# The first quarter of each batch normalisation is centred ahead of its power, and one high part moves to VectorE

## The chip, the cores and the metric

The kernel runs on one core of one Trainium2 chip. The metric is the device time of one execution in microseconds: the median of three runs. One execution was also profiled, and all rows below come from it. Names: PE is TensorE, DVE is VectorE, ACT is ScalarE, POOL is GpSimd, SP is SyncE, and PEld is TensorE's loading of weights.

## The reference, cut to what matters

The input is 8 images of 64 channels and 16 x 16 pixels. Four layers follow each other: two attention layers, a block with two batch normalisations and two convolutions with binary weights, and a whitening layer. The change touches the third and, slightly, the fourth.

```python
def batch_norm(x, gamma, beta):
    mean = jnp.mean(x, axis=(0, 2, 3), keepdims=True)
    var = jnp.mean((x - mean) ** 2, axis=(0, 2, 3), keepdims=True)
    xhat = (x - mean) * jax.lax.rsqrt(var + EPS)
    return xhat * gamma[None, :, None, None] + beta[None, :, None, None]

out = jax.nn.relu(batch_norm(x, gamma0, beta0))
shortcut = x
out = conv3x3(out, quantize_w1bit(w0))        # E * sign(w), E = mean(|w|)
out = jax.nn.relu(batch_norm(out, gamma1, beta1))
out = conv3x3(out, quantize_w1bit(w1))
return out + shortcut
# then layer 4: a mean, a 4x4 covariance per channel group, its Cholesky factor,
# a triangular solve, a mix with small weights and a bias
```

## The kernel before, in words

**Layout.** The 128 partitions hold 2 groups of 64 channels (`lanes(0)` and `lanes(1)`), each with 4 of the 8 images. The free dimension is 1024 columns: 4 quarters of 256, so one quarter is one image of each group. Every engine has its own queue of instructions, written out by hand in program order; semaphores are the only link between them. No planner orders anything.

**Attention** ends with a loop over eight units on every engine. In its tail DVE adds the shortcut of unit 6 and unit 7 (`add_shortcut`, L846), takes statistics of each quarter (L852), and between them computes for both normalisations a power of two from gamma and beta (`power_of_two`, L783 to L789), which POOL needs for the binary weights (`taps`, L373).

**A normalisation** (n = 0 on the attention's output in SBUF, n = 1 on the first convolution's output in PSUM) runs so. DVE aggregates the statistics (L923), PE combines both groups (`combine`, L666 and L667), DVE forms the variance (L929, L931), POOL raises it to the power -1/2 (L380), and DVE forms a scale `bn_s` (L935) and a shift `bn_b` (L936). Meanwhile DVE takes the absolute sums of the weights of both convolutions (`weight_sum`, L800), which PE averages (L721).

**The inputs of the convolution** are split, because the matmul reads 16-bit operands: for each quarter and each group there is a high part (the normalised, clipped value rounded to 16 bits) and a low part (the 32-bit value less the high part). They go into padded tiles `conv_in`, the high part into one half of the partitions and the low part into the other. For quarter 0, ACT writes both high parts (L473, L479) while DVE computes the 32-bit value (L902, then clipping in L903) and both low parts (L911). For quarters 1 to 3, ACT writes the clipped 32-bit value `act32` (L476) and the high part of group 1 (L479); DVE copies the high part of group 0 (L906) and subtracts its low part (L911); POOL subtracts the low part of group 1 (L386). In the second normalisation, quarter 0 was first copied out of PSUM by ACT (`z0`, L457).

**The convolution** of a quarter (`conv`, L675) is 18 matmuls and starts when its low parts are there: `lo0_out` from DVE, and `lo1_first` from DVE for quarter 0 or `lo1_out` from POOL for the others. PE works through the quarters in order. `keep_warm` (L527) fills PE's waits with matmuls of zeros. Between the convolutions, DVE takes statistics of each quarter of the first (L918). In the second, DVE takes the statistics of quarter 0 (L961, L962) between the parts of quarters 1 and 2, and PE averages them ahead of quarter 2 (L735); ACT waits for that before it centres the shortcut (L484, L488).

**After it** DVE adds the shortcut (L968), PE transposes the four quarters (L700), ACT copies each out (L494), PE multiplies each with itself (`gram`, L708), and a chain of small steps on DVE leads to the final weights and four last matmuls (L764).

Of the kernel before, what the change touches and what calls it, by code (L numbers as in the profile page):

```python
# [22 lines left out]
P = 128  # L23
B, C, H, W = 8, 64, 16, 16
G = 2
# [87 lines left out]
def build(nc, x, attn_w, params, consts, select, conv_w, out):  # L113
    with ExitStack() as ctx:
# [43 lines left out]
        z0 = sb("z0", [P, N])  # L158
# [67 lines left out]
        var_out, rstd_out, bn_out = sem("var_out"), sem("rstd_out"), sem("bn_out")  # L226
        act_out, hi0_out, hi1_out = sem("act_out"), sem("hi0_out"), sem("hi1_out")
        lo0_out, lo1_out, lo1_first = sem("lo0_out"), sem("lo1_out"), sem("lo1_first")
# [87 lines left out]
        def _(pool):  # L316
# [58 lines left out]
            for n in range(2):  # L375
# [6 lines left out]
                for q in range(1, PAIRS):  # L382

                    pool.wait_ge(act_out, n * (PAIRS - 1) + q)
                    pool.wait_ge(hi1_out, n * PAIRS + q + 1)
                    nc.gpsimd.tensor_tensor(padded(conv_in[n][1], lanes(0), q), img(act32[lanes(1), quarter(q)]),  # L386
                                            padded(conv_in[n][1], lanes(1), q), ALU.subtract).then_inc(lo1_out, 1)
# [5 lines left out]
        def _(act):  # L393
# [59 lines left out]
            for n in range(2):  # L453
                if n == 1:

                    act.wait_ge(stats_out, 1)
                    nc.scalar.activation(z0[:], pb_conv[0][0][:, 0:N], ACT.Identity).then_inc(z0_out, 1)  # L457
                act.wait_ge(bn_out, n + 1)
                for q in range(PAIRS):
                    src = xs[LAYERS][:, quarter(q)] if n == 0 else pb_conv[0][q][:, 0:N]  # L460
                    if n == 1 and q == 0:
                        act.wait_ge(z0_out, 1)
                        src = z0[:]
                    if n == 1:

                        act.wait_ge(lo0_out, q + 1)
                        if q >= 1:
                            act.wait_ge(lo1_out, q)
                    if q == 0:

                        act.wait_ge(pads_set, 4)
                        rows = lanes(0)
                        nc.scalar.activation(padded(conv_in[n][0], rows, q), img(src[rows]), ACT.Relu,  # L473
                                             scale=bn_s[n][rows], bias=bn_b[n][rows]).then_inc(hi0_out, 1)
                    else:
                        nc.scalar.activation(act32[:, quarter(q)], src, ACT.Relu, scale=bn_s[n][:],  # L476
                                             bias=bn_b[n][:]).then_inc(act_out, 1)
                    rows = lanes(1)
                    nc.scalar.activation(padded(conv_in[n][1], rows, q), img(src[rows]), ACT.Relu,  # L479
                                         scale=bn_s[n][rows], bias=bn_b[n][rows]).then_inc(hi1_out, 1)  # L480
# [31 lines left out]
        def _(pe):  # L512
# [199 lines left out]

            keep_warm(WARM[0], pb_q)
# [5 lines left out]
            pe.wait_ge(wabs_out, 2)  # L719
            for n in range(2):  # L720
                last = mm(pb_mean[:, n:n + 1], kst[:, K_ONES:K_ONES + P], wabs[n][:],  # L721
                          start=True, stop=True)
            last.then_inc(e_mm, 1)
# [43 lines left out]
        def _(dve):  # L767
# [101 lines left out]
            for i in range(ITERS):  # L869
# [24 lines left out]
            def parts(n, q):  # L894

                if q == 0:
                    dve.wait_ge(bn_out, n + 1)
                    src = xs[LAYERS][:, quarter(0)] if n == 0 else z0[:]
                    if n == 1:
                        dve.wait_ge(z0_out, 1)  # L900
                        dve.wait_ge(lo1_first, 1)
                    step(ve.tensor_scalar(act32[:, quarter(0)], src, bn_s[n][:], bn_b[n][:], ALU.mult, ALU.add))  # L902
                    step(ve.tensor_scalar(act32[:, quarter(0)], act32[:, quarter(0)], 0.0, None, ALU.max))  # L903
                else:
                    dve.wait_ge(act_out, n * (PAIRS - 1) + q)
                    ve.tensor_copy(padded(conv_in[n][0], lanes(0), q),  # L906
                                   img(act32[lanes(0), quarter(q)])).then_inc(hi0_out, 1)
                for g in range(G if q == 0 else 1):
                    hi_out, lo_out = ((hi0_out, lo0_out), (hi1_out, lo1_first))[g]
                    dve.wait_ge(hi_out, n * PAIRS + q + 1)  # L910
                    ve.tensor_tensor(padded(conv_in[n][g], lanes(1 - g), q),  # L911
                                     img(act32[lanes(g), quarter(q)]), padded(conv_in[n][g], lanes(g), q),
                                     ALU.subtract).then_inc(lo_out, 1)
# [6 lines left out]
            for n in range(2):  # L920
# [3 lines left out]
                if n == 0:  # L924
                    weight_sum(0)
# [6 lines left out]
                if n == 0:  # L932
                    weight_sum(1)
                dve.wait_ge(rstd_out, n + 1)
                step(ve.tensor_tensor(bn_s[n][:], t[:, 4:5], rstd[n][:], ALU.mult))  # L935
                ve.scalar_tensor_tensor(bn_b[n][:], pb_small[:, 0:1], bn_s[n][:], t[:, 5:6], ALU.mult, ALU.subtract,  # L936
# [154 lines left out]
```

## Time and profile before

| what | value |
|---|---|
| median of 3 runs | 80.1 us (79.8, 80.1, 80.28) |
| the profiled execution, whole | 79.73 us |
| its span (first to last instruction) | 77.6 us |
| busy, PE / DVE / ACT / POOL | 82% / 67% / 59% / 31% |
| granted TensorE clock | 9 tenths or more in all 40 slices |
| chain that ended last, by engine | PE 47%, DVE 23%, ACT 15%, issue 6%, POOL 5% |

The profiled execution is 2.13 us longer than its span, time that lies ahead of the first and behind the last instruction. PE's busy share contains the zero matmuls of `keep_warm`: the largest single group of the profile is those, with 17.3 us. The busy shares are means over stages with different limits, so the stage from 43 to 67 us has to be read by its chain of waits.

### The profile page before, as it was taken

Reading aid. Unit: us, or ns where it says so; the run is one execution under the profiler, and the core shown is the slowest. Engines: PE = TensorE matmul, PEld = TensorE weight load, DVE = VectorE, ACT = ScalarE, POOL = GpSimd, SP = SyncE. Lnnn points to the kernel's source line nnn. Section 1 sums busy time; section 2 is a strip of 40 time slices with the busy share of each in tenths; the row PEclk is TensorE's granted clock in tenths of the full one; section 3 lists DMA queues with packets and bytes.
Section 4 is the critical chain, followed back from the end, with each engine's and each line's share of the span. In section 5 each row is a group of like instructions: output and inputs, shape, how many; then the busy total and the mean of one; then the engine's idle time right before and its main releaser. Section 6 shows DMA issues by size and latency. Waiting matters only on the chain.

```text
span 77.6 us, 1563 instructions
## 1 busy us (share of the span) xinstructions
PE 63.9 (82%) x507; PEld 36.5 (47%) x510; DVE 52.2 (67%) x141; ACT 46.1 (59%) x131; POOL 24.0 (31%) x60
## 2 busy tenths in 40 slices
PE   3997975499989998969398898897978999899640
PEld 1463533163636353526234446674527866453620
DVE  1058994847988898879871988995486962368340
ACT  4201647989898989899866029950099883113130
POOL 7005038603849384630333020540204600002000
PEclk9999999999999999999999999999999999999999
DMA  0898800000000000000000000000000000000033
GB/s 9 209 241 250 324 6 0 0 0 0 0 8 4 0 0 0 0 8 0 8 0 0 0 0 0 0 0 8 0 0 0 0 0 0 8 0 0 0 135 136
DMA packets 2456, 2.63 MB, mean 34 GB/s; under 512 B 401, under 2 KB 2065, under 8 KB 2449
## 3 DMA queue, kind: packets, MB, share of 16 engines
q1 hardware_dynamic: 2304, 2.48, 10.3%
q8 instruction: 4, 0.07, 0.4%
q10 hardware_dynamic: 144, 0.07, 0.3%
q14 instruction: 4, 0.02, 0.1%
HBM read 2.02 MB, written 0.52 MB: 33 GB/s over the span
## 4 chain that ended last, share of the span: by engine, by line
PE 47%; DVE 23%; ACT 15%; issue 6%; POOL 5%; POOLq 1%; DVEq 0%; ACTq 0%
PE bank L675 9%; PE bank L624 9%; ACT bank L413 7%; PE bank L537 4%; PE bank L527 4%; DVE cut L818 3%; PE bank L561 3%; DVE negmax L808 3%; PE bank L608 3%; PE bank L764 2%; ACT conv_in L479 2%; PE bank L593 2%; PE bank L700 2%; DVE qk L832 2%; POOL conv_in L386 2%
## 5 line engine op out<-in xcount | busy, mean ns | idle before, releaser
L527 PE MATMUL bank<-warm 128*128 128x512 bf16 x65 | 17.3, 402 | 1.5 <-DVE warm L777 1.2
L413 ACT ACTIVATE bank<-bank,negmax 128x256 f32<-128x256 f32 x32 | 14.3, 447 | 2.3 <-DVE negmax L808 2.0
L675 PE MATMUL bank<-conv_in,taps 128*64 128x256 f16 x144 | 9.9, 278 | 1.5 <-DVE conv_in L911 0.7
L808 DVE TENSOR_REDUCE negmax<-bank 128x2 f32<-128x512 f32 x16 | 10.3, 684 | 1.2 <-PE bank L577 1.1
L527 PEld LDWEIGHTS bank<-warm 128*128 128x128 bf16 x68 | 6.6, 104 | 8.7 <-issue 2.3
L624 PE MATMUL bank<-probs,vt 128*64 128x256 f32 x64 | 9.1, 391 | 0.5 <-ACT probs L426 0.5
L675 PEld LDWEIGHTS bank<-conv_in,taps 128*64 128x64 bf16 x144 | 7.5, 109 | 3.2 <-issue 3.1
L426 ACT ACTIVATE probs<-bank 128x512 f32<-128x512 f32 x16 | 8.6, 589 | 0.7 <-PE bank L598 0.7
L818 DVE TENSOR_SCALAR cut<-bank,prm 128x256 f32<-128x256 f32 x8 | 3.9, 482 | 5.0 <-PE bank L537 5.0
L386 POOL TENSOR_TENSOR conv_in<-act,conv_in 64x256 f16<-64x256 f32 x6 | 4.1, 681 | 8.2 <-ACT conv_in L479 8.2
L413 ACT ACTIVATION_READ_ACCUMULATOR bank<-bank,negmax 128x1 f32 x32 | 6.6, 205 | 0.0
L832 DVE CAST qk<-bank 128x512 bf16<-128x512 f32 x8 | 5.5, 685 | 1.1 <-PE bank L547 1.1
L329 POOL TENSOR_TENSOR cut<-cut 64x256 f32<-64x256 f32 x7 | 4.3, 611 | 5.8 <-DVE cut L818 4.6
L342 POOL TENSOR_TENSOR shift<-negmax,lntot 128x4 f32<-128x4 f32 x8 | 1.6, 203 | 13.3 <-ACT lntot L418 13.3
L624 PEld LDWEIGHTS bank<-probs,vt 128*64 128x64 f32 x64 | 4.5, 136 | 2.6 <-issue 0.8
L608 PE MATMUL bank<-half,shift 128*128 128x128 f16 x16 | 2.3, 224 | 4.0 <-POOL shift L349 3.1
L537 PE MATMUL bank<-x,aw 128*128 128x256 f32 x16 | 5.5, 423 | 0.0
L911 DVE TENSOR_TENSOR conv_in<-act,conv_in 64x256 f16<-64x256 f32 x10 | 4.9, 492 | 0.3
L434 ACT ACTIVATE shift_t<-bank 128x256 bf16<-128x256 f32 x8 | 3.1, 383 | 3.3 <-PE bank L608 3.2
L332 POOL TENSOR_TENSOR cut<-cut 32x256 f32<-32x256 f32 x7 | 4.3, 611 | 0.5
L838 DVE COPY vt<-bank 128x256 f32<-128x256 f32 x8 | 3.4, 422 | 0.7 <-PE bank L561 0.2
L577 PE MATMUL bank<-qk 64*128 64x256 bf16 x32 | 3.1, 274 | 0.8 <-DVE qk L832 0.7
(124 smaller groups left out, 100.9 us busy)
## 6 DMA issues: line engine op xcount, KB each, us to landing
cw<-conv_w SPq DMA_DIRECT2D x2, 288.0 KB, 4.0
x<-x_in SPq DMA_DIRECT2D x4, 128.0 KB, 2.6
out<-res SPq DMA_DIRECT2D x4, 128.0 KB, 1.9
kst<-consts SPq DMA_DIRECT2D x1, 386.5 KB, 4.6
aw<-attn_w SPq DMA_DIRECT2D x2, 128.0 KB, 2.7
half<-select SPq DMA_DIRECT2D x1, 96.0 KB, 2.6
kst<-consts SPq DMA_DIRECT2D x1, 64.5 KB, 2.9
aw<-attn_w ACTq DMA_DIRECT2D x1, 64.0 KB, 2.5
```

The lines of the kernel that those rows point to most:

```text
L386: nc.gpsimd.tensor_tensor(padded(conv_in[n][1], lanes(0), q), img(act32[lanes(1), quarter(q)]), padded(conv_in[n][1], lanes(1), q), ALU.su ...
L413: nc.scalar.activation(part, part, ACT.Exp, bias=negmax[:, i % 2, n:n + 1], accum_out=total[:, i % 2, n:n + 1]).then_inc(total_out, 1)
L426: nc.scalar.activation(probs[:, i % 2, g], pb_t[g][:].rearrange("p (t n) -> p t n", t=CH), ACT.Exp).then_inc(exp_out, 1)
L527: mm(bank[:], warm[:, 0:P], warm[:], start=True, stop=True)
L537: mm(proj(i), aw[:, w:w + P], x_of(i), start=True, stop=True).then_inc(proj_mm, 1)
L608: last = mm(pb_rows[:, u * P:(u + 1) * P], tops[:, u, 1::2], half[:, 0, :], start=True, stop=True)
L624: last = mm(mixed(i)[g * C:(g + 1) * C], vt[:, i % 2, t, g * C:(g + 1) * C], probs[:, i % 2, g, t, :], start=(t == 0), stop=(t == CH - 1))
L675: last = mm(img(pb_conv[n][q][lanes(g), 0:N]), taps[n][:, k, :], conv_in[n][g][:, q, dy:dy + H, dx:dx + W], start=(k == 0), stop=(k == TAP ...
L808: ve.tensor_reduce(negmax[:, i % 2, g * CH:(g + 1) * CH], pb_s[(2 * i + g) % 3][:].rearrange("p (t n) -> p t n", t=CH), AX.X, ALU.max, neg ...
L818: ve.tensor_scalar(cut[:, i], proj(i), prm[:, bias:bias + 1], None, ALU.add).then_inc(part0_out, 1)
L832: ve.tensor_copy(qk[:, i].rearrange("p o n -> p (o n)"), pb_rep[:]).then_inc(qk_out, 1)
L911: ve.tensor_tensor(padded(conv_in[n][g], lanes(1 - g), q), img(act32[lanes(g), quarter(q)]), padded(conv_in[n][g], lanes(g), q), ALU.subtr ...
```

## The change

Both absolute sums of the weights move into the tail of attention, ahead of each `power_of_two`, and PE's average of them moves ahead of the zero matmuls before the first `combine`. DVE reads that average before it waits for the combination. While POOL computes the power, DVE copies the mean out of PSUM and writes quarter 0 less its mean to a buffer `z0`, of which there are now two. ACT then starts quarter 0's high parts as soon as the scale is there, with beta as its bias; ACT's copy of quarter 0 out of PSUM is gone. DVE computes the 32-bit value of quarter 0 from the centred one, then the shift for the other quarters, and takes the low parts with one operation that clips and subtracts. In quarter 1, DVE and not ACT writes the high part of group 1, ahead of the one of group 0. In the second normalisation the high part of quarter 2 is taken ahead of the statistics. PE does the third transpose ahead of the first gram, and the fourth ahead of the second.

```diff
-        z0 = sb("z0", [P, N])
+        z0 = [sb(f"z0{n}", [P, N]) for n in range(2)]
+        mean = [sb(f"mean{n}", [P, 1]) for n in range(2)]
...
                 for q in range(1, PAIRS):
                     pool.wait_ge(act_out, n * (PAIRS - 1) + q)
-                    pool.wait_ge(hi1_out, n * PAIRS + q + 1)
+                    if q == 1:
+                        pool.wait_ge(hi1_dve, n + 1)
+                    else:
+                        pool.wait_ge(hi1_out, n * (PAIRS - 1) + q)
...
-                if n == 1:
-                    act.wait_ge(stats_out, 1)
-                    nc.scalar.activation(z0[:], pb_conv[0][0][:, 0:N], ACT.Identity).then_inc(z0_out, 1)
-                act.wait_ge(bn_out, n + 1)
-                for q in range(PAIRS):
+                act.wait_ge(scale_out, n + 1)
+                act.wait_ge(z0_out, n + 1)
+                act.wait_ge(pads_set, 4)
+                beta = bn_t[n][:, 5:6]
+                for g, hi_out in enumerate((hi0_out, hi1_out)):
+                    rows = lanes(g)
+                    nc.scalar.activation(padded(conv_in[n][g], rows, 0), img(z0[n][rows]), ACT.Relu,
+                                         scale=bn_s[n][rows], bias=beta[rows]).then_inc(hi_out, 1)
+                act.wait_ge(shift0_set, n + 1)
+                for q in range(1, PAIRS):
...
+                    nc.scalar.activation(act32[:, quarter(q)], src, ACT.Relu, scale=bn_s[n][:],
+                                         bias=bn_b[n][:]).then_inc(act_out, 1)
+                    if q >= 2:
+                        rows = lanes(1)
+                        nc.scalar.activation(padded(conv_in[n][1], rows, q), img(src[rows]), ACT.Relu,
+                                             scale=bn_s[n][rows], bias=bn_b[n][rows]).then_inc(hi1_out, 1)
...
+            pe.wait_ge(kst_in, 16)
+            pe.wait_ge(wabs_out, 2)
+            for n in range(2):
+                last = mm(pb_mean[:, n:n + 1], kst[:, K_ONES:K_ONES + P], wabs[n][:],
+                          start=True, stop=True)
+            last.then_inc(e_mm, 1)
             keep_warm(WARM[0], pb_q)
...
             transposed(1)
+            transposed(2)
             gram(0)
-            transposed(2)
+            transposed(3)
             gram(1)
-            transposed(3)
             gram(2)
...
                     for n in range(2):
+                        weight_sum(n)
                         power_of_two(n)
...
+            def first_inputs(n):
+                if n == 1:
+                    dve.wait_ge(lo1_first, 1)
+                step(ve.tensor_scalar(act32[:, quarter(0)], z0[n][:], bn_s[n][:], bn_t[n][:, 5:6],
+                                      ALU.mult, ALU.add))
+                ve.scalar_tensor_tensor(bn_b[n][:], mean[n][:], bn_s[n][:], bn_t[n][:, 5:6], ALU.mult, ALU.subtract,
+                                        reverse1=True).then_inc(shift0_set, 1)
+                for g, (hi_out, lo_out) in enumerate(((hi0_out, lo0_out), (hi1_out, lo1_first))):
+                    dve.wait_ge(hi_out, n * (PAIRS, PAIRS - 1)[g] + 1)
+                    ve.scalar_tensor_tensor(padded(conv_in[n][g], lanes(1 - g), 0),
+                                            img(act32[lanes(g), quarter(0)]), 0.0,
+                                            padded(conv_in[n][g], lanes(g), 0),
+                                            ALU.max, ALU.subtract).then_inc(lo_out, 1)
+
+            def high_parts(n, q):
+                dve.wait_ge(act_out, n * (PAIRS - 1) + q)
+                if q == 1:
+                    ve.tensor_copy(padded(conv_in[n][1], lanes(1), q),
+                                   img(act32[lanes(1), quarter(q)])).then_inc(hi1_dve, 1)
+                ve.tensor_copy(padded(conv_in[n][0], lanes(0), q),
+                               img(act32[lanes(0), quarter(q)])).then_inc(hi0_out, 1)
+
+            def low_part(n, q):
+                dve.wait_ge(hi0_out, n * PAIRS + q + 1)
+                ve.tensor_tensor(padded(conv_in[n][0], lanes(1), q), img(act32[lanes(0), quarter(q)]),
+                                 padded(conv_in[n][0], lanes(0), q), ALU.subtract).then_inc(lo0_out, 1)
...
                 if n == 0:
-                    weight_sum(0)
+                    dve.wait_ge(e_mm, 1)
+                    step(ve.tensor_copy(emean[:], pb_mean[:, 0:2]))
+                    step(ve.tensor_tensor(esq[:], emean[:, 0:1], emean[:, 0:1], ALU.mult))
                 dve.wait_ge(comb_mm, n + 1)
...
                 ve.tensor_tensor(var[n][:], pb_small[:, 1:2], var[n][:], ALU.add).then_inc(var_out, 1)
+                step(ve.tensor_copy(mean[n][:], pb_small[:, 0:1]))
+                src = xs[LAYERS][:, quarter(0)] if n == 0 else pb_conv[0][0][:, 0:N]
+                ve.tensor_scalar(z0[n][:], src, mean[n][:], None, ALU.subtract).then_inc(z0_out, 1)
+                dve.wait_ge(rstd_out, n + 1)
+                ve.tensor_tensor(bn_s[n][:], t[:, 4:5], rstd[n][:], ALU.mult).then_inc(scale_out, 1)
+                dve.wait_ge(scale_out, n + 1)
+                dve.wait_ge(z0_out, n + 1)
+                dve.wait_ge(pads_set, 4)
+
+                first_inputs(n)
+                high_parts(n, 1)
+                low_part(n, 1)
                 if n == 0:
+                    step(ve.tensor_scalar(esq[:], esq[:], E_SQUARE_MIN, None, ALU.max))
+                    high_parts(0, 2)
+                    low_part(0, 2)
                     conv0_statistics(0)
                     step(ve.reciprocal(einv[:], esq[:]))
+                    high_parts(0, 3)
+                    low_part(0, 3)
...
                 else:
+                    high_parts(1, 2)
                     dve.wait_ge(conv_mm, PAIRS + 1)
                     step(ve.bn_stats(stats[2][:], pb_conv[1][0][:, 0:N]))
                     ve.bn_aggr(mv[2][:], stats[2][:]).then_inc(bn_v, 1)
-                    parts(1, 2)
-                    parts(1, 3)
+                    low_part(1, 2)
+                    high_parts(1, 3)
+                    low_part(1, 3)
```

## Rows read from the trace of the kernel before

**Rows 1.** Chain of waits, first normalisation: start us, length us, engine, tile, line.

```profile
45.80 0.23 DVE bn_b L936
...
46.06 0.60 ACT conv_in L473
...
49.50 1.21 PE bank L675 x18
...
53.23 0.44 DVE stats L918
```

**Rows 2.** Chain of waits, second normalisation, second convolution and grams.

```profile
55.99 0.23 DVE bn_b L936
...
59.62 1.21 PE bank L675 x18
...
61.14 1.14 PE bank L675 x18
...
66.08 0.39 ACT yt L494
...
66.52 0.48 PE bank L708 x8
```

**Rows 3.** Timeline of DVE, attention's tail: start, busy us, line, operation [idle before].

```profile
39.81 0.48 DVE L846 SCALAR_TENSOR_TENSOR x<-bank,prm,x 128x256 f32<-128x256 f32 x1 [0.38 <-PE bank L624]
...
42.57 0.48 DVE L846 SCALAR_TENSOR_TENSOR x<-bank,prm,x 128x256 f32<-128x256 f32 x1 [1.61 <-PE bank L624]
```

**Rows 4.** Timeline of PE, from attention's end to the first convolution.

```profile
42.47 1.04 PE L527 MATMUL bank<-warm 128*128 128x512 bf16 x4
...
47.14 0.50 PE L721 MATMUL bank<-wabs,kst 128*128 128x1 f32 x4
47.93 0.30 PE L675 MATMUL bank<-conv_in,taps 128*64 128x256 f16 x2 [0.29 <-DVE conv_in L911]
```

**Rows 5.** Timeline of DVE, first normalisation.

```profile
44.85 0.74 DVE L800 TENSOR_REDUCE wabs<-cw 128x1 f32<-128x576 f32 x1
...
46.13 0.41 DVE L902 TENSOR_SCALAR act<-x,bn_s,bn_b 128x256 f32<-128x256 f32 x1
46.58 0.29 DVE L903 TENSOR_SCALAR act<-act 128x256 f32<-128x256 f32 x1
...
47.94 0.29 DVE L906 CAST conv_in<-act 64x256 f16<-64x256 f32 x1 [0.16 <-ACT act L476]
...
48.72 0.16 DVE L945 COPY emean<-bank 128x2 f32<-128x2 f32 x1
```

**Rows 6.** Timeline of POOL, both normalisations.

```profile
45.02 0.56 POOL L380 TENSOR_TENSOR rstd<-var,kst 128x1 f32<-128x1 f32 x1 [2.21 <-DVE var L931]
...
48.70 0.65 POOL L386 TENSOR_TENSOR conv_in<-act,conv_in 64x256 f16<-64x256 f32 x1 [3.13 <-ACT conv_in L479]
49.92 0.74 POOL L386 TENSOR_TENSOR conv_in<-act,conv_in 64x256 f16<-64x256 f32 x1 [0.57 <-ACT conv_in L479]
...
59.97 0.72 POOL L386 TENSOR_TENSOR conv_in<-act,conv_in 64x256 f16<-64x256 f32 x1 [0.50 <-ACT conv_in L479]
```

**Rows 7.** Timeline of DVE beside those of POOL, both normalisations.

```profile
48.92 0.45 DVE L946 TENSOR_TENSOR esq<-emean 128x1 f32<-128x1 f32 x1
...
49.73 0.42 DVE L911 TENSOR_TENSOR conv_in<-act,conv_in 64x256 f16<-64x256 f32 x1
...
59.36 0.43 DVE L961 BATCH_NORM_STATS2 stats<-bank 128x6 f32<-128x256 f32 x1 [0.52 <-PE bank L675]
59.83 0.18 DVE L962 BATCH_NORM_AGGREGATE mv<-stats 128x2 f32<-128x6 f32 x1
59.92 0.26 DVE L906 CAST conv_in<-act 64x256 f16<-64x256 f32 x1
60.21 0.77 DVE L911 TENSOR_TENSOR conv_in<-act,conv_in 64x256 f16<-64x256 f32 x1
```

**Rows 8.** Timeline of ACT, second normalisation.

```profile
57.50 0.56 ACT L476 ACTIVATE act<-bank,bn_b,bn_s 128x256 f32<-128x256 f32 x1
```

More of the change, by code:

```diff
@@ L225, in build @@
         comb_mm = sem("comb_mm")
-        var_out, rstd_out, bn_out = sem("var_out"), sem("rstd_out"), sem("bn_out")
+        var_out, rstd_out = sem("var_out"), sem("rstd_out")
+        scale_out, shift0_set = sem("scale_out"), sem("shift0_set")
         act_out, hi0_out, hi1_out = sem("act_out"), sem("hi0_out"), sem("hi1_out")
+        hi1_dve = sem("hi1_dve")
         lo0_out, lo1_out, lo1_first = sem("lo0_out"), sem("lo1_out"), sem("lo1_first")
@@ L460, in _ @@
+                act.wait_ge(shift0_set, n + 1)
+                for q in range(1, PAIRS):
                     src = xs[LAYERS][:, quarter(q)] if n == 0 else pb_conv[0][q][:, 0:N]
-                    if n == 1 and q == 0:
-                        act.wait_ge(z0_out, 1)
-                        src = z0[:]
                     if n == 1:
                         act.wait_ge(lo0_out, q + 1)
[L467 to L477, printed above, removed]
@@ L478, in _ @@
-                    rows = lanes(1)
-                    nc.scalar.activation(padded(conv_in[n][1], rows, q), img(src[rows]), ACT.Relu,
-                                         scale=bn_s[n][rows], bias=bn_b[n][rows]).then_inc(hi1_out, 1)
+                        act.wait_ge(lo1_out, q)
+                    nc.scalar.activation(act32[:, quarter(q)], src, ACT.Relu, scale=bn_s[n][:],
[4 more added lines that the diff above has]
+                                             scale=bn_s[n][rows], bias=bn_b[n][rows]).then_inc(hi1_out, 1)
@@ L717, in _ @@
             keep_warm(WARM[1], pb_q)
[L719 to L723, printed above, removed]
             pe.wait_ge(taps_out, 1)
@@ L892, in _ @@
             dve.wait_ge(kst_in, 16)
[L894 to L913, printed above, removed]
@@ L931, in _ @@
                 ve.tensor_tensor(var[n][:], pb_small[:, 1:2], var[n][:], ALU.add).then_inc(var_out, 1)
-                if n == 0:
[L933 to L936, printed above, removed]
-                                        reverse1=True).then_inc(bn_out, 1)
-                dve.wait_ge(pads_set, 4)
@@ L940, in _ @@
-                parts(n, 0)
-                parts(n, 1)
-                if n == 0:
-                    dve.wait_ge(e_mm, 1)
-                    step(ve.tensor_copy(emean[:], pb_mean[:, 0:2]))
-                    step(ve.tensor_tensor(esq[:], emean[:, 0:1], emean[:, 0:1], ALU.mult))
-                    parts(0, 2)
+                step(ve.tensor_copy(mean[n][:], pb_small[:, 0:1]))
+                src = xs[LAYERS][:, quarter(0)] if n == 0 else pb_conv[0][0][:, 0:N]
+                ve.tensor_scalar(z0[n][:], src, mean[n][:], None, ALU.subtract).then_inc(z0_out, 1)
@@ L948, in _ @@
                     conv0_statistics(0)
-                    parts(0, 3)
-                    step(ve.tensor_scalar(esq[:], esq[:], E_SQUARE_MIN, None, ALU.max))
                     step(ve.reciprocal(einv[:], esq[:]))
+                    high_parts(0, 3)
+                    low_part(0, 3)
                     step(ve.tensor_scalar(eps1[:], einv[:], BN_EPS, None, ALU.mult))
                     conv0_statistics(1)
+                    ve.tensor_scalar(nscale[:], emean[:, 1:2], -1.0, None, ALU.mult).then_inc(pivot_set, 1)
@@ L954, in _ @@
+                    ve.tensor_scalar(nxm[:], mean[0][:], -1.0, None, ALU.mult).then_inc(pivot_set, 1)
                     conv0_statistics(2)
-                    ve.tensor_scalar(nscale[:], emean[:, 1:2], -1.0, None, ALU.mult).then_inc(pivot_set, 1)
-                    ve.tensor_scalar(nxm[:], pb_small[:, 0:1], -1.0, None, ALU.mult).then_inc(pivot_set, 1)
                     conv0_statistics(3)
                 else:
+                    high_parts(1, 2)
                     dve.wait_ge(conv_mm, PAIRS + 1)
```

## The prediction

> **What bounds the kernel now.** I read the chain of waits first, from attention's end to the grams, then the timelines of DVE, POOL, ACT and PE over the same stretch, to see what each does while another is waited for. In the chain, each normalisation is a serial ladder: the shift on DVE ends at 46.03, ACT starts its first high part at 46.06, POOL's low part of quarter 1 starts at 48.70 and PE's quarter 1 at 49.50 [rows 1, 6]. The second has the same steps ten microseconds later, 55.99 and 59.62 [rows 2]. From 59.62 on PE is the chain, quarter after quarter; conv(1,2) starts at 61.14 less what is merged there, by my reading of the gaps 61.07. It ends in the grams, where the last waits for ACT's copy (66.08, then 66.52) [rows 2]. PE's quarters take 1.21 us each. The engine that looks idle in the totals is POOL, but it matters here for what it holds.
>
> **What holds what.** A 64-partition subtraction of two SBUF tiles takes DVE 0.42 us when POOL is quiet, but 0.77 us when it starts at 60.21 while POOL's runs from 59.97 to 60.69: it ends 0.29 us behind POOL's end. One of a single column, started at 48.92 beside POOL's 48.70 to 49.35, takes 0.45 us and ends 0.02 behind it [rows 6, 7]. So such an operation asks for something of POOL's about 0.13 us after its start, waits for POOL's end, and then does the rest. The other way, POOL's takes 0.65 us alone [rows 6], but 0.74 us when DVE's subtraction of 49.73 still runs for 0.23 us of it: it asks about 0.14 us in. The one of 59.97 takes 0.72 us, and beside its start there is a DVE cast (59.92, 0.26 us), not a subtraction [rows 6, 7]. If it asks at 60.11 and the cast holds until 60.18, the 0.07 us are explained. So I take casts of SBUF tiles, and the fast column operations (a 256-column one takes 0.29 us, less than the 0.42 us of a subtraction [rows 5, 7]), to hold and be held too. The trace has no cast that starts well inside a POOL operation; that is the open price of this forecast, bounded below.
> The Trainium skill ("SBUF — State Buffer", section "Who interferes with whom") says that DVE and POOL share one pair of SBUF ports as an exclusive lock; two-input operations contend with a POOL operation that reads, and so do `copy`, `cast` and `tensor_scalar` in their two-port modes, and the second to come "fully blocks". On two-input operations the trace agrees (0.77 against 0.42 us); on casts it shows only the 0.07 us. By the rule the sum is the one below; without it for one-input operations it is rival A's.
>
> **Part 1, weight sums and PE's average moved.** Two reductions at 0.74 us each [rows 5] go in front of DVE's unit 6, which waited 0.38 us [rows 3]: it is 1.48 - 0.38 = 1.10 us later, at 40.9. Its only follower that counts is unit 7 at 42.57, which had 1.61 us of idle before it [rows 3]: 0.5 us are left. Cost 0. If that cover failed, each excess would go one for one into the first normalisation. In their old place the sums cost nothing either (0.74 us from 44.85 ends at 45.59, POOL's power at 45.58 [rows 5, 6]). PE's average, 0.50 us [rows 4], moves in front of 4 zero matmuls; PE idled from their end at 43.51 to 43.87, so `combine` could be up to 0.14 us late if a modelled end is a real one; the matmul behind a zero one starts some 0.17 us before that end (47.14 against 44.34 + 2.97 = 47.31 for the 13 later ones). I take 0, bounds 0 and +0.14. DVE's two small steps on the average (0.16 us each, [rows 5]) fit in its wait for `combine`.
>
> **Part 2, centring under the power.** DVE adds a copy of the mean (0.16 us, as the one of 48.72 [rows 5]) and z0. In n = 1 z0 reads PSUM: a 256-column operation from PSUM with a column operand is 0.48 us [rows 3]; 55.06 + 0.16 + 0.03 + 0.48 ends at 55.7, just within the power (which ended at 55.77 and gave `bn_s` 55.80 to 55.97; [rows 2] has the step behind it). In n = 0 it reads SBUF: between 0.29 us (no column operand) and 0.41 us (two of them) [rows 5], so 0.35. It starts at 45.04 and asks for what POOL holds after the power has, which started at 45.02 and ends at 45.58 [rows 6]. Held until then, with 0.13 left, it ends at 45.71, and `bn_s` starts at 45.74 instead of 45.61: +0.13. Bounds: 0 (not held) and +0.22 (all but the first 0.13 left).
> What goes is the shift before ACT's start: 0.23 us and its gap, 0.25 us in each [rows 1, 2]. So ACT starts 0.12 us earlier in n = 0. ACT's two high parts take 1.22 us and DVE's last low part comes behind them: at 47.62 instead of 47.79, conv(0,0) at 47.76 instead of 47.93 [rows 4]. The clip folded away (0.29 us [rows 5]) only made the low parts late by 0.05; they now wait for ACT. The value's operation (0.41) and the shift (0.23) end at 46.7, long before the shift is read at 47.19: cost 0.
>
> **Part 3, DVE takes a high part.** ACT's high part of quarter 1 (0.60) falls out of POOL's path; DVE's cast (0.29 [rows 5]) stands in. In n = 0: act32 ready at 47.79, first cast to 48.11, POOL from 48.27 to 48.94 (held 0.02 by the second cast, which runs to 48.43). Quarter 1 on POOL's side is then ready at 49.07, 0.43 earlier. But DVE's subtraction starts at 48.47, asks at 48.60, 0.19 after POOL (48.41), and is held to 48.94 + 0.29 = 49.23. conv(0,1) starts at 49.36 against 49.50 [rows 1]: -0.14. In the kernel before it was through before POOL began.
> Behind it on DVE's queue: esq (0.15, to 49.41), the cast of quarter 2 (held by POOL's next, 49.20 to 49.85, to 50.01), its subtraction to 50.47, ready at 50.60 against PE's 50.57. Statistics (0.43), reciprocal (0.16), cast and subtraction of quarter 3, ready at 51.92 against PE's 51.81. The convolution ends at 53.12 against 53.20: **-0.08**.
>
> **Part 4, the second normalisation**, all times with that -0.08. ACT starts at 55.92 and POOL's quarter 1 at 58.20, until 58.87; DVE's subtraction is held to 59.16; conv(1,1) at 59.29 against 59.62 [rows 2]: -0.33. Then DVE's queue: the cast of quarter 2 is now ahead of the statistics. It starts at 59.19, POOL's quarter 2 (from 59.05) holds it to 59.70 + 0.16 = 59.86; statistics 0.43 and aggregation 0.18 [rows 7] to 60.54; the subtraction of quarter 2 starts at 60.45 and asks at 60.58, but POOL's quarter 3 runs from 60.22 (ACT's four parts of 0.56 [rows 8] and their gaps end at 60.06) to 60.87. Held: 61.16. conv(1,2) starts at 61.29 against 61.07: **+0.22**. The combination behind the statistics (60.58) is earlier than before (60.76) and hidden. Quarter 3 is ready at 62.07, long before PE's 62.69.
>
> **Part 5, transposes.** The last gram waited some 0.10 us (66.43 to 66.52) for ACT's copy [rows 2]. With the transposes ahead PE runs through: **-0.10**; no transpose waits, since yc of quarter 3 is there 0.6 us before it is needed. Bounds: -0.15 and 0.
>
> **Sum.** -0.08 at the first convolution's end becomes +0.22 at conv(1,2), and -0.10: +0.12 us. The profiled execution took 79.73, so 79.85; the median shown lies 0.37 above that execution, so 80.2. The gains of 0.25 us per normalisation and 0.43 on POOL's path are real, and are given back on DVE's queue.
>
> **Rivals.**
> A. Not held when it has one input: z0 and the casts run free (for: no cast in the trace is lengthened, the 0.26 us one even beside POOL; against: POOL's 0.72 us). Then `bn_s` starts at 45.61 and conv(0,1) at 49.21, still behind a held subtraction: -0.29, kept to the end of the convolution. In n = 1 conv(1,1) is 0.56 early, the cast of quarter 2 ends at 59.25, statistics and aggregation at 59.93, and the subtraction asks at 59.97, ahead of POOL's 60.15; conv(1,2) is 0.56 early. With part 5: -0.66, 79.07; median 79.4.
> B. Nothing is held in the new places (POOL yields to DVE or the operations miss each other). Then quarter 1 waits for neither: -0.58 in n = 0, as much again in n = 1, and -0.10: about -1.25, median 78.9. Against: rows of 60.21 and 48.92 [rows 7].
> C. Slower. A held operation of one input begins afresh once POOL is through. Price: z0 +0.09 more, each of the two held casts of quarter 2 +0.13, and z0's and the first cast's shift all of the DVE-bound chain; with late `combine` (+0.14) the sum is +0.12 + 0.09 + 0.26 + 0.14 = +0.6, median 80.7. It is slower by over 0.5% once these holds cost 0.28 us more than I took. Against: the held two-input ones paid only their remainder.
> D. The change doesn't do what it says: z0 ends so late (+0.22 and more) that ACT starts no earlier, and the rest evens out: 0, median 80.1.
>
> **Chances.** My forecast 0.46, A 0.19, B 0.11, C 0.17, D 0.07. This kernel's measurement can tell about 0.5%, 0.4 us, from no change. The forecast gives 0.37 same, 0.04 faster, 0.05 slower; A 0.17 faster and 0.02 same; B 0.11 faster; C 0.17 slower; D 0.07 same. Faster 0.32, same 0.46, slower 0.22. The range must hold A and C with the runs' own scatter (0.3 below the median, 0.2 above), and leaves out most of B: 79.1 to 80.8. The forecast's own range is 79.8 to 80.5.
>
> **What the changed profile would show.** z0 of n = 0 at about 0.66 us, that of n = 1 at 0.48; ACT's first high part 0.1 us earlier in n = 0; DVE's subtraction of quarter 1 at about 0.75 us in both normalisations and not 0.42; the cast of quarter 2 at over 0.5 us; PE idle before conv(1,2), with DVE as the releaser; the grams without a gap. A cast of 0.29 us in the middle of a POOL operation means A. Subtractions of 0.42 us throughout mean B. If unit 7's shortcut starts later than 42.57, part 1 has cost something and the forecast is wrong there.

## The result, and the profile after

The changed kernel took 79.48 us (median of 9 runs, 78.72 to 79.84) against 80.28 us before (9 runs), ratio 0.9889, interval 0.984 to 0.9938. The time is inside the stated range, and below the forecast's own 79.8 to 80.5: the kernel got faster by 1.1% where no change, and in the sum +0.12 us, was forecast. A second measurement, on one chip with some of the experiments, gave 0.9803 (0.9754 to 0.9853), where I expected 0.987.

The two profiled executions cannot be compared by their spans (77.6 and 77.4 us). The start, which the change does not touch, differs: the first projection takes 0.77 us before and 1.06 us after, though the granted clock reads 1.00 in both stretches, and what follows is shifted. First PE of the kernel before, then of the changed one:

```profile
3.70 0.77 PE L537 MATMUL bank<-x,aw 128*128 128x256 f32 x2
...
7.23 0.39 PE L577 MATMUL bank<-qk 64*128 64x256 bf16 x4 [0.35 <-DVE qk L832]
```

```profile
3.71 1.06 PE L537 MATMUL bank<-x,aw 128*128 128x256 f32 x2
...
7.75 0.39 PE L577 MATMUL bank<-qk 64*128 64x256 bf16 x4 [0.35 <-DVE qk L833]
```

So I count from the shortcut of unit 7 on DVE (42.57 before [rows 3], 43.13 after), the last thing ahead of the normalisations. Of the 0.56 us between these two, 0.52 already stand at the rows of 7.23 and 7.75, long before any instruction that the change moves. From the shortcut on, kernels with the same work agree within 0.03 us (the two profiles of the changed kernel within 0.01), while the runs of one kernel scatter over more than 1 us. By "stages" I mean this stretch. The table gives the start of each quarter of the convolutions (conv01 is quarter 1 of the first, conv12 quarter 2 of the second), the aggregation that opens the second normalisation, and the start of `gmask`, the first operation behind the grams:

```
us after unit 7's shortcut  conv00 conv01  aggr. conv10 conv11 conv12 conv13  gmask  outside
before                        5.36   6.93  11.12  15.54  17.05  18.50  19.90  24.45   2.15
changed                       5.13   6.65  10.81  14.94  16.42  18.29  19.70  23.72   1.82
changed, second profile       5.13   6.66  10.81  14.94  16.42  18.29  19.69  23.71   1.82
e1 transposes only            5.35   6.92  11.11  15.52  17.03  18.49  19.89  23.91   2.16
e2 transposes undone          5.13   6.65  10.82  14.95  16.43  18.29  19.68  24.24   1.81
e3 high part on ACT           5.14   6.75  10.94  15.07  16.61  18.07  19.47  23.49   1.98
e9 casts exchanged            5.13   6.91  10.80  14.93  16.67  18.13  19.53  23.55   1.81
e5 POOL only writes           5.14    -    10.40  14.52    -    17.19  18.59  22.62   1.77
e8 low part first             5.14   6.67  10.82  14.95  16.44  17.58  19.51  23.66   1.79
b1 no meeting in quarter 1    5.14   6.54  11.04  15.18  16.54    -    19.73  23.89   1.79
```

"Outside" is the time of an execution less its span, the mean over a kernel's runs (its single runs: 2.11 to 2.21 in the kernel before, 1.76 to 1.88 in the changed one; e9 and e5 have one run each); a dash is a start that the trace merges with the quarter before (conv12 of e8 is counted from such a merged row, see there). The stages give 24.45 - 23.72 = 0.73 us and the time outside 0.33, together 1.06 us, 1.3%, a ratio of 0.987. That is inside the first interval and just above the end of the second, 0.9853. In the second measurement three of the eight runs (79.76 to 79.92 us) count as slow and are left out of its ratio; the means of all runs, 79.22 against 80.42 us, are 1.5% apart.

DVE in the changed kernel, first normalisation, then second (start, busy us, line, operation):

```profile
43.13 0.48 DVE L847 SCALAR_TENSOR_TENSOR x<-bank,prm,x 128x256 f32<-128x256 f32 x1 [0.64 <-PE bank L624]
...
45.66 0.35 DVE L948 TENSOR_SCALAR z<-x,mean 128x256 f32<-128x256 f32 x1
46.23 0.16 DVE L950 TENSOR_TENSOR bn_s<-bn_t,rstd 128x1 f32<-128x1 f32 x1 [0.22 <-POOL rstd L383]
...
48.96 0.77 DVE L923 TENSOR_TENSOR conv_in<-act,conv_in 64x256 f16<-64x256 f32 x1
...
49.95 0.45 DVE L917 CAST conv_in<-act 64x256 f16<-64x256 f32 x1
...
58.74 0.76 DVE L923 TENSOR_TENSOR conv_in<-act,conv_in 64x256 f16<-64x256 f32 x1
59.53 0.63 DVE L917 CAST conv_in<-act 64x256 f16<-64x256 f32 x1
...
60.75 0.62 DVE L923 TENSOR_TENSOR conv_in<-act,conv_in 64x256 f16<-64x256 f32 x1
```

POOL beside it:

```profile
45.64 0.56 POOL L383 TENSOR_TENSOR rstd<-var,kst 128x1 f32<-128x1 f32 x1 [2.27 <-DVE var L945]
48.78 1.47 POOL L392 TENSOR_TENSOR conv_in<-act,conv_in 64x256 f16<-64x256 f32 x2 [2.58 <-ACT act L475]
...
58.56 1.46 POOL L392 TENSOR_TENSOR conv_in<-act,conv_in 64x256 f16<-64x256 f32 x2 [2.54 <-ACT act L475]
60.43 0.65 POOL L392 TENSOR_TENSOR conv_in<-act,conv_in 64x256 f16<-64x256 f32 x1 [0.41 <-ACT conv_in L479]
```

DVE's subtraction of quarter 1 in the kernel before:

```profile
48.27 0.42 DVE L911 TENSOR_TENSOR conv_in<-act,conv_in 64x256 f16<-64x256 f32 x1
```

What had been 0.42 us there, in both normalisations, is now 0.77 and 0.76. The casts of quarter 2, before 0.29 us in the first normalisation and 0.26 in the second [rows 7], are 0.45 and 0.63. The subtraction of 60.75 ends at 61.37, 0.29 us behind POOL's 60.43 + 0.65. But z0 of the first normalisation runs its 0.35 us inside POOL's power without being held. PE:

```profile
59.55 1.21 PE L675 MATMUL bank<-conv_in,taps 128*64 128x256 f16 x18 [0.27 <-DVE conv_in L923]
60.77 0.38 PE L736 MATMUL bank<-mv,kst 128*128 128x1 f32 x2
61.42 1.22 PE L675 MATMUL bank<-conv_in,taps 128*64 128x256 f16 x18 [0.27 <-DVE conv_in L923]
...
64.46 0.66 PE L700 MATMUL bank<-kst,yc 128*128 128x128 f32 x4
65.05 0.45 PE L708 MATMUL bank<-yt 128*64 128x65 f32 x8
65.47 0.41 PE L700 MATMUL bank<-kst,yc 128*128 128x128 f32 x2
65.81 1.00 PE L708 MATMUL bank<-yt 128*64 128x65 f32 x24
```

The third quarter waits 0.27 us for DVE, which it did not before. Twenty-four gram matmuls run in one stretch of 1.00 us.

### The profile page after: what moved, and what is told of

It is laid out like the page before. It is cut to its first block, busy times and chain, and to the rows that moved or that the text cites. A ratio compares the mean times of both kernels' runs of the same rounds, so it can differ in the third digit from the quotient of the medians.

```text
span 77.4 us, 1565 instructions
## 1 busy us (share of the span) xinstructions
PE 64.1 (83%) x506; PEld 36.4 (47%) x510; DVE 53.5 (69%) x145; ACT 44.2 (57%) x128; POOL 24.2 (31%) x60
## 4 chain that ended last, share of the span: by engine, by line
PE 47%; DVE 23%; ACT 13%; issue 8%; POOL 4%; POOLq 1%; DVEq 0%; ACTq 0%
PE bank L624 9%; ACT bank L419 7%; PE bank L527 6%; PE bank L537 5%; PE bank L675 5%; PE bank L561 3%; DVE negmax L809 3%; PE bank L608 3%; DVE conv_in L917 3%; DVE conv_in L923 2%; PE bank L765 2%; PE bank L593 2%; DVE cut L819 2%; DVE qk L833 2%; ACT conv_in L466 2%
## 5 line engine op out<-in xcount | busy, mean ns | idle before, releaser
L466 ACT ACTIVATE conv_in<-z,bn_t,bn_s 64x256 f16<-64x256 f32 x4 | 2.4, 601 | 9.5 <-DVE bn_s L950 9.5
L537 PEld LDWEIGHTS bank<-x,aw 128*128 128x128 f32 x16 | 3.1, 222 | 2.2 <-issue 1.8
```

The source lines that it names most:

```text
L537: mm(proj(i), aw[:, w:w + P], x_of(i), start=True, stop=True).then_inc(proj_mm, 1)
```

## The experiments

**The order of transposes and grams.** e1 is the kernel before with this alone, e2 the changed kernel without it.

```diff
             transposed(1)
+            transposed(2)
             gram(0)
-            transposed(2)
+            transposed(3)
             gram(1)
-            transposed(3)
             gram(2)
```

> The kernel before, with only the order of transposes and grams changed. Theory: with the third and fourth transposes ahead, 24 gram matmuls run at a stretch, and the stretch from the second transpose to the end of the grams falls from 2.9 to about 2.35 us, so -0.5 us, a ratio of 0.994; the unhidden copy of the fourth quarter had cost 0.27 us of it, and the changes between transposes and grams the rest. Rival (my prediction's term): only the gap of 0.1 us goes, ratio 0.999.

> The changed kernel with the old order of transposes and grams. Theory: the normalisations leave only -0.2 us at the third quarter of the second convolution, so the ratio to the kernel before is about 0.9975, and the stretch from the second transpose to the end of the grams is 2.9 us again. Rival: the normalisations carry most of the gain, ratio 0.992.

Measured: e1 ratio 0.9913 (0.9873 to 0.9954), stages -0.54 us, all of it behind conv13. e2 ratio 0.988 (0.9825 to 0.9935), stages -0.21 us; the rest of its time is the 0.34 outside and, by its span, scatter of the start, so its ratio alone would have misled. In e2 the last two grams show what the order costs:

```profile
65.69 0.44 PE L700 MATMUL bank<-kst,yc 128*128 128x128 f32 x2
66.06 1.00 PE L708 MATMUL bank<-yt 128*64 128x65 f32 x16
```

Sixteen matmuls, with the wait for ACT's copy in them, take the same 1.00 us as twenty-four without it. So eight behind each other are worth (1.00 - 0.45) / 2 = 0.28 us, and the wait was 0.27 us, not the 0.10 that I took. The new order also has two changes between transposes and grams less (three in place of five). By this estimate they are the other 0.27 us, some 0.13 each; no run has them alone. The theory holds, and the term is 0.54 us.

The chain of waits of the kernel before shows where my 66.43 came from: 65.30 is the start of a gram, 65.68 of the transposes behind it, and I gave the next gram the same 0.38 us.

```profile
65.30 0.38 PE bank L708 x8
```

**The high part of quarter 1.** e3 gives it back to ACT:

```diff
-                    if q == 1:
-                        pool.wait_ge(hi1_dve, n + 1)
-                    else:
-                        pool.wait_ge(hi1_out, n * (PAIRS - 1) + q)
+                    pool.wait_ge(hi1_out, n * PAIRS + q + 1)
...
-                    if q >= 2:
+                    if q >= 1:
                         rows = lanes(1)
...
-                if q == 1:
-                    ve.tensor_copy(padded(conv_in[n][1], lanes(1), q),
-                                   img(act32[lanes(1), quarter(q)])).then_inc(hi1_dve, 1)
```

> The changed kernel, with ScalarE writing the high part of group 1 in quarter 1 as before, all else kept. Theory (the early high part is given back because VectorE's subtraction meets GpSimd's): VectorE's subtraction of quarter 1 takes 0.42 us again instead of 0.77; the second quarter of the first convolution starts at most 0.1 us later, and the third quarter of the second convolution starts 0.1 to 0.2 us EARLIER against the statistics' end than in the changed kernel; time equal to the changed kernel's within 0.2 us, ratio to before 0.987 to 0.991. Rival (the moved high part is a true gain of 0.3 us per normalisation): slower than the changed kernel by 0.4 us or more, ratio 0.994.

Ratio to before 0.9819 (0.9753 to 0.9885), 79.46 us: the same time as the changed kernel. In the stages it is 0.23 us shorter at `gmask`, 0.22 at conv12; outside the span it is 0.16 us longer (1.98 against 1.82), so that 0.07 us are left. Its subtraction of quarter 1 is free again:

```profile
48.88 0.42 DVE L916 TENSOR_TENSOR conv_in<-act,conv_in 64x256 f16<-64x256 f32 x1
...
58.78 0.42 DVE L916 TENSOR_TENSOR conv_in<-act,conv_in 64x256 f16<-64x256 f32 x1
```

So the moved high part gains 0.10 and 0.19 us at conv01 and conv11 and loses more at conv12. This part of the change is a loss in the stages, as the theory said; the runs cannot tell so little.

**Who asks first.** e9 keeps DVE's two casts and exchanges them, so POOL starts one cast later:

```diff
+                ve.tensor_copy(... conv_in[n][0] ...).then_inc(hi0_out, 1)
                 if q == 1:
                     ve.tensor_copy(... conv_in[n][1] ...).then_inc(hi1_dve, 1)
-                ve.tensor_copy(... conv_in[n][0] ...).then_inc(hi0_out, 1)
```

> The changed kernel with VectorE's two casts of quarter 1 exchanged, so that GpSimd starts 0.33 us later, just behind VectorE's subtraction. Theory (whoever asks first holds the other): VectorE's subtraction of quarter 1 takes 0.42 us, GpSimd's takes 0.80 instead of 0.66; the second quarter of the first convolution starts 6.9 us after unit 7's shortcut instead of 6.65, the third quarter of the second within 0.15 us of the changed kernel's 18.29. If the price lay in VectorE's queue and not in who asks first, the subtraction would stay at 0.76.

DVE in e9, second normalisation, and POOL beside it:

```profile
58.45 0.42 DVE L923 TENSOR_TENSOR conv_in<-act,conv_in 64x256 f16<-64x256 f32 x1
58.91 0.63 DVE L914 CAST conv_in<-act 64x256 f16<-64x256 f32 x1
```

```profile
58.59 2.46 POOL L392 TENSOR_TENSOR conv_in<-act,conv_in 64x256 f16<-64x256 f32 x3 [2.86 <-DVE conv_in L917]
```

The same operation behind the same two casts takes 0.42 us where it took 0.76, since it now starts 0.14 us before POOL's and not 0.18 behind it. Now POOL is the one that is held: its first subtraction takes 0.80 us of that row (forecast 0.80), against 0.66 in the changed kernel, and PE's quarter 1 waits for it. So the order decides who pays, and DVE's price was the higher one. In the first normalisation the hold moves on: there DVE's subtraction of quarter 2 takes 0.76 us (0.43 in the changed kernel). The second convolution's third quarter, conv12, starts at 18.13, and conv01 at 6.91 (forecast 6.9); 18.13 is 0.01 outside the forecast's window of 18.14 to 18.44. PE waits more for quarter 1 and less for quarter 2.

**Reading taken away.** e5 has POOL write zeros where it subtracted:

```diff
-                    nc.gpsimd.tensor_tensor(padded(conv_in[n][1], lanes(0), q), ...
+                    nc.gpsimd.memset(padded(conv_in[n][1], lanes(0), q), 0.0).then_inc(lo1_out, 1)
```

> The changed kernel; GpSimd's low parts of group 1 in quarters 1 to 3 are left out, zeros are written in their place, so GpSimd reads nothing there. Theory (VectorE's subtraction and casts are held by GpSimd's reading subtraction, and this is what gives the gain back): VectorE's subtractions take 0.42 us in every quarter, and the third quarter of the second convolution starts about 17.4 us after unit 7's shortcut, against 18.29 in the changed kernel and 18.50 before. If the casts are held by any GpSimd operation, also one that only writes, some of them are still above 0.29 us. Rival (VectorE's queue is simply too long): still above 18.0 with subtractions of 0.42 us.

DVE, then POOL, in the second normalisation of e5:

```profile
58.13 0.29 DVE L916 CAST conv_in<-act 64x256 f16<-64x256 f32 x1
58.45 0.42 DVE L922 TENSOR_TENSOR conv_in<-act,conv_in 64x256 f16<-64x256 f32 x1
58.91 0.49 DVE L916 CAST conv_in<-act 64x256 f16<-64x256 f32 x1
```

```profile
58.24 0.43 POOL L392 MEMSET conv_in<- 64x256 f16 x1 [2.52 <-ACT act L474]
58.94 0.31 POOL L392 MEMSET conv_in<- 64x256 f16 x1 [0.27 <-ACT conv_in L478]
```

conv12 starts at 17.19 us, 1.10 earlier (forecast 17.4), and the one run took 78.17 us. Some of that is POOL's shorter operation, which also makes quarter 1 ready earlier; the queue on DVE is the same, so its length alone is not the price. The subtraction is not held by an operation that only writes, the cast is (0.49 against 0.29 us), and it holds one in turn (0.43 against 0.31). The first of these readings rests on 0.09 us: held until POOL's end at 58.67, the subtraction would have taken 0.51 us. With the casts of the changed kernel (0.45 and 0.63 us) this is the measurement that the first profile lacked. It bears out the Trainium skill, "SBUF — State Buffer", section "Who interferes with whom", on both kinds; the power in the next experiment is a case that does not follow its rule of two SBUF inputs beside a POOL operation that reads.

**The centring beside the power.** e4 writes z0 as an operation of two SBUF inputs:

```diff
-                ve.tensor_scalar(z0[n][:], src, mean[n][:], None, ALU.subtract).then_inc(z0_out, 1)
+                    ve.tensor_tensor(z0[n][:], src, mean[n][:].to_broadcast([P, N]), ALU.subtract)...
```

> The changed kernel, with the centring of the first normalisation written as a subtraction of two SBUF tiles (the mean broadcast), which the profile shows to be held beside GpSimd's subtractions. It runs beside GpSimd's power. If the power holds what GpSimd's 256-column subtraction holds, and only one-input operations were free of it, z0 takes 0.8 us and the scale is 0.3 us later. If GpSimd's power of one column holds nothing for most of its 0.56 us, z0 takes 0.42 us.

```profile
46.06 0.45 DVE L949 TENSOR_TENSOR z<-x,mean 128x256 f32<-128x256 f32 x1
```

POOL's power ran from 46.05 to 46.61. Even an operation of two SBUF inputs is not held here, and the power is not lengthened either (0.56 us, as in the kernel before), so it is not that z0 came first. The power holds nothing for most of its time, whatever the number of inputs. One reserve: the second input is a single column read over and over, and no row shows such an operation beside a subtraction. The stages are those of the changed kernel.

**Weight sums and the time outside the span.** e7 is the kernel before with part 1 alone; e12 moves DVE's sums and leaves TensorE's average; e13 moves the first sum only; e10 and e11 add what else had changed in number. The excerpt shows the line that e7 and e12 add (in e13 for n = 0 only), then e10's and e11's; the sums in their old place go, and e7 moves the average as the change does.

```diff
                     for n in range(2):
+                        weight_sum(n)
                         power_of_two(n)
...
+        unused = [sem("unused0"), sem("unused1")]
...
+            pe.wait_ge(kst_in, 16)
             keep_warm(WARM[0], pb_q)
```

> The kernel before, with only the weight sums and their average moved. Theory: no stage gets shorter: the first convolution starts 5.36 us after unit 7's shortcut as before (PE not free earlier than the low parts), so the span is unchanged. The time outside the span, 2.13 to 2.15 us before and 1.8 in the changed kernel, stays at 2.15 if it doesn't depend on this part, and falls to 1.8 if it does.

> The kernel before with two more semaphores that nothing uses. The time outside the span is 2.15 us before (57 semaphores less two of the changed one), 1.98 in the variant with one semaphore more, 1.82 in the changed kernel with two more. Theory: it follows the number of semaphores, so 1.8 us here. Rival: it follows the instructions, so 2.15 here.

> The kernel before with the weight sums moved on VectorE, but TensorE's average left in its old place. Stages as in the kernel before (the end of the grams 24.45 us after unit 7's shortcut). If the 0.26 us less outside the span, seen with both moved, comes from VectorE's part, it is here too (1.9 us); if from TensorE's, it is 2.15 us. Span equal to before within 0.2 us if the 0.4 us less of span with both moved was scatter of the start.

> The kernel before with one more, long fulfilled, wait on TensorE ahead of the first combination. Stages as before. If one more instruction in TensorE's queue sets the time outside the span, that is 1.9 us; if not, 2.15 us.

> The kernel before with only the first convolution's weight sum moved into attention's tail on VectorE. Stages unchanged (end of the grams 24.45 us after unit 7's shortcut). The time outside the span is 2.15 us before and 1.88 with both sums moved; in between (2.0) if it goes with the amount moved, one of the two if it goes with the place of one of them.

All five have the stages of the kernel before within 0.02 us. Outside the span: e7 1.90 us (8 runs), e12 1.88 (10), e13 1.81 (one run), e10 2.15 (8), e11 2.16 (8). The guess on semaphores is refuted, and so is an instruction more on TensorE. The drop goes with the place of the sums on DVE, and by the one run of e13 with that of the first alone. The 1.98 us of e3, which has both sums moved, shows that something else acts on it too. By time, e7 0.9923 (0.9887 to 0.996), e12 0.9967 (0.9929 to 1.0006), e10 1.0003 (0.9943 to 1.0062), e11 1.0036 (0.9997 to 1.0075). The mean spans are 77.8 for e7 against 78.2 before and 78.3 for e12 against 78.3: what e7 has beyond 0.26 us is most likely the start's scatter, since its stages are the old ones. Why the place of a sum moves time outside the span stays open.

**The way to a better one.** e8 takes DVE's low part of quarter 2 out from behind the statistics, and PE's average of these goes behind the first four taps. b1 has that too, and avoids all meetings in quarter 1: ACT writes its high part of group 1, and DVE takes both of its low parts. The excerpt is e8's.

```diff
                     high_parts(1, 2)
+                    low_part(1, 2)
                     dve.wait_ge(conv_mm, PAIRS + 1)
...
-                    low_part(1, 2)
...
+            inputs_ready(1, 2)
+            conv_taps(1, 2, range(0, 4))
             pe.wait_ge(bn_v, 3)
             mm(pb_small[:, 0:1], kst[:, K_AVG:K_AVG + P], mv[2][:, 0:1], ...
-            conv(1, 2)
+            conv_taps(1, 2, range(4, TAPS))
```

> The changed kernel, but in the second normalisation VectorE takes the low part of quarter 2 ahead of the statistics of quarter 0, and TensorE averages these after the first 4 taps of that quarter. Theory (the third quarter of the second convolution is late because its low part stands behind the held cast and the statistics, and then meets GpSimd once more): the low part asks 0.25 us ahead of GpSimd's third, takes 0.42 us instead of 0.61 and is ready when TensorE is; the third quarter starts 17.6 us after unit 7's shortcut (18.29 in the changed kernel), the grams end at 23.1 to 23.2 (23.72), ratio to the kernel before 0.979 to 0.981. Rival (the late average makes ScalarE's centring the bound, as with the candidate that had no meetings): the gain at the third quarter is lost again before the transposes, the grams end at 23.7.

> A candidate better than both, on the theory that the ports are the price: the changed kernel, but ScalarE writes the high part of group 1 in quarter 1, VectorE takes both low parts of quarter 1 (GpSimd takes none there), VectorE takes the low part of quarter 2 ahead of the statistics in the second normalisation, and TensorE averages these after the first 4 taps of that quarter. By the theory no operation of quarter 1 is held (0.42 us each), the second quarter of the first convolution starts 6.5 us after unit 7's shortcut (6.65 in the changed kernel, 6.75 with the high part on ScalarE), the third quarter of the second at 17.5 to 17.7 (18.29, 18.07), and the time is 0.5 to 0.7 us under the changed kernel's: ratio to the kernel before 0.980. Rival (VectorE's queue length decides): the extra 0.45 us on VectorE per normalisation make it no faster than the changed kernel, 18.3.

e8: DVE and PE, second normalisation:

```profile
59.66 0.43 DVE L925 TENSOR_TENSOR conv_in<-act,conv_in 64x256 f16<-64x256 f32 x1
...
62.25 1.27 DVE L986 SCALAR_TENSOR_TENSOR yc<-bank,emean,xc 128x256 f32<-128x256 f32 x3 [0.85 <-ACT xc L488]
```

```profile
59.02 1.77 PE L675 MATMUL bank<-conv_in,taps 128*64 128x256 f16 x26 [0.27 <-DVE conv_in L925]
60.83 0.38 PE L738 MATMUL bank<-mv,kst 128*128 128x1 f32 x2
```

The low part asks first and is 0.43 us; quarter 2 follows quarter 1 without a gap (26 matmuls in one stretch), at 59.02 + 1.14 - 42.58 = 17.58 (1.14 us from one quarter to the next, as in [rows 2]), as the theory said (17.6). So the place behind the held cast and the statistics was what held conv12. But the second half of the forecast failed, and the rival's holds. Of the 0.71 us gained at conv12, 0.52 are gone at conv13: the average, which used to run in PE's gap, now costs its 0.3 us in the convolution, and before it PE waits for the statistics, which now stand behind the low part. The average starts 18.25 us after the shortcut, 0.61 later than in the changed kernel (17.64), and DVE then waits 0.85 us for ACT's centring, which takes 0.13 more. At `gmask` 0.06 us are left; ratio 0.9888 (0.9828 to 0.9948), forecast 0.979 to 0.981. b1 has the same end (DVE waits 1.41 us for ACT there) and another: with the high part on ACT and POOL behind it, its quarter 2 of the first convolution waits 0.27 us for POOL. Stages 23.89, ratio 0.9856 (0.9816 to 0.9896), forecast 0.980: no better than the changed kernel. Neither beats it; e3 and e9 are 0.2 us shorter in the stages, which the runs cannot confirm.

## Why the prediction was wrong

- **Part 5 was mis-sized**, and is the largest miss: -0.10 forecast, -0.54 measured. I took the wait for ACT's copy as the gap from 66.43 to 66.52; 66.43 stands in no row of [rows 2], it is a start of 66.05 and 0.38 us per gram, a pitch that holds only where each gram stands between transposes. Behind each other they take 0.28, so my gap hid most of the wait. The changes between transposes and grams were no term at all.
- **Part 2, z0 held by the power**, +0.13 forecast, 0 measured (0.35 us; 0.45 with two inputs). I carried the rule from POOL's subtraction over to its power, which no row showed. (Even by that rule the sum was off: of 0.35 us all but the first 0.13 would have been left, so +0.22.) The convolution's end is -0.31 instead of -0.08: 0.13 of that is z0, and the other 0.10 is that quarters 2 and 3 did not come late by what I had added for them.
- **Part 3 was right**: the subtraction of quarter 1 meets POOL's and takes 0.77 us in place of 0.42, the cast of quarter 2 is held, and PE's gain on POOL's side is given back. e3, e9 and e5 show it. Forecast for conv01 -0.14, measured -0.28, the difference being mostly z0. Two small misses cancel in it: the variance starts 0.06 us later after the shortcut than before (2.01 against 1.95), and PE follows DVE's subtraction by 0.05 us where I took 0.13.
- **Part 4 was right in its mechanism; its gain was put too low and its loss too high**: conv11 -0.33 forecast, -0.63 measured; then 0.55 us were to be lost until conv12, and 0.42 were. DVE releases PE there, as forecast. The sign at conv12 came out the other way, -0.21 and not +0.22, since 0.23 of the 0.43 us lie in the first normalisation.
- **Part 1 costs nothing in the stages**, as forecast (unit 7 had 0.64 us of its 1.61 of idle left, and `combine` starts 1.29 us after the shortcut, before 1.30). The sign that I had named against it, a shortcut later than 42.57, did appear (43.13), but 0.52 of its 0.56 us stand at the start of the kernel already. Its 0.26 us outside the span were no term of mine, and with the rest 0.33. The prediction added what lies around the span as a constant, and it was not.
- **The sum**: the misses of 0.44, 0.43 and 0.33 us make 1.20, against 1.18 between +0.12 and -1.06. Rival A came nearest in time (79.4), and that is luck: it was right that z0 is not held, but its casts are, it took my 0.10 us for the grams, and it had nothing outside the span. Rival B's condition is refuted by the 0.77 us subtraction, and D's by ACT, which starts 0.19 us earlier (3.30 against 3.49 us after the shortcut). Rival C's, that held operations begin afresh, is refuted by the 0.45 us cast: it ends 0.15 us behind POOL's end (50.25), not 0.29.

## What to carry to other kernels

Before work moves from one engine to another in parallel with a third, lay out who asks first for what they share: 0.30 us in POOL's start decided here on 0.34 us of hold on DVE, and the price that DVE was spared went in part to POOL. Take the price of a wait between short matmuls from a stretch where they run without it, not from the gap in the rows. And where runs scatter by 1 us, count stages from a common event: they repeat to 0.03 us and show what the times cannot.

## What was not expected of the hardware

- POOL's power on one column (0.56 us) holds neither a 256-column operation of one SBUF input (0.35 us) nor one of two (0.45 us), while its 256-column subtraction (0.65 us) holds both kinds (0.77 and 0.63 us).
- The time outside the span went from 2.15 to 1.88 us when two sums moved some 6 us earlier on DVE; the cause is open.
- The first projection took between 0.67 (e8) and 1.06 us in executions with the same work and a granted clock of 1.00, and unit 7's shortcut began between 42.57 and 43.88 us. The two profiles of the changed kernel differ by 0.75 us there and by 0.7 in their spans, so in these two the scatter lies ahead of the shortcut.
